# First cross attention: values projected in their own batch, keys a batch ahead, first context and weights split beside the query projection

## The reference

```python
def _L0_xattn_ref(Q, K, V, mask, Wq, bq, Wk, bk, Wv, bv, Wo, bo):
    q = _split_heads(Q @ Wq + bq)          # 16 heads of 32
    k = _split_heads(K @ Wk + bk)
    v = _split_heads(V @ Wv + bv)
    logits = jnp.einsum('bhqd,bhkd->bhqk', q, k) / jnp.sqrt(jnp.float32(DEPTH))
    logits = logits + mask * -1000000000.0
    attn = jax.nn.softmax(logits, axis=-1)
    ctx = jnp.einsum('bhqk,bhkd->bhqd', attn, v)
    ctx = ctx.transpose(0, 2, 1, 3).reshape(Q.shape[0], Q.shape[1], DIM)
    return ctx @ Wo + bo
x = x + _L0_xattn_ref(_layernorm(x, axis=-1), ctx_1024, ctx_1024, mask, ...)
```

## Time and profile before

| | |
|---|---|
| median of three runs | 1742.85 us |
| the profiled execution | 1742.32 us |
| its span | 1740.5 us |
| busy: TensorE / VectorE / ScalarE / GpSimd | 1498.8 (86%) / 1121.7 (64%) / 594.0 (34%) / 295.8 (17%) us |
| first cross attention with query projection | 19.7 to 664 us of the span |
| mean granted clock of TensorE | 0.939 of 2.4 GHz |

### The profile page before, as it was taken

How to read it: one execution, slowest core, us unless ns; L and a number is a source line. 1 busy time by engine, 2 the same in 40 slices (tenths; PEclk the granted TensorE clock), 3 DMA queues, 4 the chain that set the end, 5 groups by cost and what they waited for, 6 DMA issues and landing times. The chain is left out here.

```text
span 1740.5 us, 34070 instructions
## 1 busy us (share of the span) xinstructions
PE 1498.8 (86%) x14116; PEld 989.4 (57%) x14130; DVE 1121.7 (64%) x2155; ACT 594.0 (34%) x1221; POOL 295.8 (17%) x185
## 2 busy tenths in 40 slices
PE   6789999999999975997675999998799995885786
PEld 3567777777777753344644444444466663675343
DVE  3366777667777666614876677574588883665575
ACT  1244444444444431231033111101466661044332
POOL 0400000000000000400010000000599982160000
PEclk9889999999999987899788999998899997898899
DMA  6113123231331214000005000000454521004001
GB/s 233 62 39 133 64 90 94 71 125 64 98 97 60 77 39 138 0 0 2 4 1 200 0 0 0 0 0 0 188 206 168 199 70 35 1 3 146 0 0 48
DMA packets 47910, 120.05 MB, mean 69 GB/s; under 512 B 10606, under 2 KB 15470, under 8 KB 43675
## 3 DMA queue, kind: packets, MB, share of 16 engines
q1 hardware_dynamic: 47770, 118.04, 19.9%
HBM read 100.95 MB, written 17.07 MB: 68 GB/s over the span
## 5 line engine op out<-in xcount | busy, mean ns | idle before, releaser
L1134 POOL TENSOR_TENSOR tm_mixed<-tm_mixed,XNT 128x512 f32<-128x512 f32 x16 | 21.8, 1383 | 648.6 <-DVE tm_mixed L1157 648.6
L478 PE MATMUL bank<-l0x_ctxT,l0x_upper_k 128*128 128x512 f32 x256 | 107.7, 421 | 5.1 <-ACT l0x_upper_k L627 5.1
L697 DVE TENSOR_SCALAR l0x_upper<-bank 128x512 int32<-128x512 int32 x64 | 44.0, 688 | 97.9 <-PE bank L460 92.4
L617 ACT ACTIVATE l0x_ctxT<-l0x_upper 128x512 fp32r<-128x512 f32 x64 | 40.4, 631 | 193.4 <-DVE l0x_ctxT_lower L700 193.4
L478 PE MATMUL bank<-l0x_upper_v,l0x_ctxT 128*128 128x512 f32 x256 | 105.6, 412 | 0.0
L478 PE MATMUL bank<-l0x_ctxT,l0x_lower_k 128*128 128x512 f32 x256 | 101.8, 398 | 0.0
L478 PE MATMUL bank<-l0x_ctxT_lower,l0x_upper_k 128*128 128x512 f32 x256 | 101.6, 397 | 0.0
L478 PE MATMUL bank<-l0x_upper_v,l0x_ctxT_lower 128*128 128x512 f32 x256 | 100.8, 394 | 0.0
L478 PE MATMUL bank<-l0x_lower_v,l0x_ctxT 128*128 128x512 f32 x256 | 100.4, 392 | 0.0
L634 ACT ACTIVATE l0x_prob<-l0x_prob,l0x_negmax 128x512 f32<-128x512 f32 x128 | 91.8, 717 | 17.6 <-DVE l0x_negmax L712 17.6
L1047 DVE TENSOR_REDUCE l1x_negmax<-bank 128x1 f32<-128x512 f32 x128 | 82.3, 685 | 21.3 <-PE bank L936 20.8
(11 more groups left out here) (264 smaller groups left out, 3363.4 us busy)
## 6 DMA issues: line engine op xcount, KB each, us to landing
l0x_ctx<-in_ctx SPq DMA_DIRECT2D x16, 1024.0 KB, 4.9
l1x_ctx<-in_ctx SPq DMA_DIRECT2D x16, 1024.0 KB, 5.8
fp_weight<-l0x_weight_piece SPq DMA_DIRECT2D x24, 352.0 KB, 2.5
f_raw<-fp_weight SPq DMA_DIRECT2D x3, 2816.0 KB, 17.4
ternary_weight<-l1x_piece_out SPq DMA_DIRECT2D x24, 256.0 KB, 6.1
f_raw<-ternary_weight SPq DMA_DIRECT2D x3, 2048.0 KB, 13.9
l0x_abs_piece<-in_L_ffn_w_gate SPq DMA_DIRECT2D x8, 512.0 KB, 5.7
l0x_mask<-mask_scratch SPq DMA_DIRECT2D x16, 256.0 KB, 3.8
```

The source lines that it names most:

```text
L478: last = nc.tensor.matmul(work[bank][:, :], stationary, moving, start=kc == 0 and i == 0, stop=kc == CH - 1 and i == 2)
L697: nc.vector.tensor_scalar(upper.bitcast(I32), work[bank][:, :].bitcast(I32), UPPER_BITS, None, ALU.bitwise_and).then_inc(ctx_upper, 1)
```

## The change

1. In `query_projection` TensorE also turns the four chunks of context 0, one after each of the query chunks 2 to 5, in two PSUM banks that the queries give up (they use six banks, and the last two chunks wait for the first two to be copied). VectorE splits Wk and Wv after the first two query chunks and context 0 after the next four; GpSimd's subtractions, ScalarE's rounding of Wk and of context 0 lie there too. The rounding of Wv is ScalarE's first step in the attention. The splits use the buffers of V, Wo takes the place of Wq.
2. Ahead of the loop stand only the four keys of batch 0 and two turns of context 1. Batch b now computes its own four values in its first half and the four keys of batch b + 1 in its second half. The four context turns are spread: two of context b + 1 in the first half, two of context b + 2 in the second.
3. The scores come half a batch at a time at the start of each half, and the four masked scores and four exponentials of a half stand together in their engines' queues; before they came two and two between other steps. The value product of the second half and the sums' turn come after the first value chunk of the next batch.
4. VectorE's quantising and magnitudes keep their amounts per step, at new places. All order is unrolled over b; SyncE's loop too.

The core of the diff (the waits and addresses that only follow the new counts are left out):

```diff
 def query_projection(nc, g, w):
...
+            for i, (weight, lower) in enumerate(((w.Wk, w.lower_k), (w.Wv, w.lower_v))):
+                pool.wait_ge(w.upper_done, i + 1)
+                nc.gpsimd.tensor_tensor(lower[:, :, :], weight[:, :, :], w.raw_upper[i], ALU.subtract).then_inc(w.lower_done, 1)
...
             for j in range(8):
...
+                if j >= 6:
+                    pe.wait_ge(done, j - 5)
...
+                if TURNS_AFTER <= j < TURNS_AFTER + CH:
+                    turn(j - TURNS_AFTER)
...
+            act.wait_ge(w.lower_done, 1)
+            nc.scalar.activation(w.upper_k[:, :, :], w.raw_upper[0], ACT.Copy).then_inc(w.weights_ready, 1)
+            for c in range(CH):
+                act.wait_ge(w.ctx_lower, c + 1)
+                nc.scalar.activation(w.ctxT[0][:, c, :], w.upper[:, :], ACT.Copy).then_inc(w.ctxt_ready, 1)
...
+                if j < 2:
+                    weight_upper(j, (w.Wk, w.Wv)[j])
+                elif TURNS_AFTER <= j < TURNS_AFTER + CH:
+                    context_parts(j - TURNS_AFTER)
...
+def work_order():
+
+    order = [("key", 0, p) for p in range(CH)] + [("turn", 1, 0), ("turn", 1, 1)]
+    for b in range(B):
+        order += [("value", b, 0), ("value", b, 1), ("turn", b + 1, 2), ("value", b, 2), ("turn", b + 1, 3), ("value", b, 3)]
+        order += [("key", b + 1, 0), ("key", b + 1, 1), ("turn", b + 2, 0), ("key", b + 1, 2)]
+        order += [("out", b // 2 - 1, 0)] if b % 2 == 0 and b > 0 else []
+        order += [("turn", b + 2, 1), ("key", b + 1, 3)]
+        order += [("out", b // 2 - 1, 1)] if b % 2 == 0 and b > 0 else []
+    order += [("out", TILES - 1, 0), ("out", TILES - 1, 1)]
+    return [use for use in order if use[0] == "out" or use[1] < B]
...
         @block.sync
...
+            for b in range(B):
+                it = b // 2
+                if b % 2 == 1:
+                    piece(it, 1)
+                if b + 3 < B:
+                    context_load(b + 3)
+                if b + 2 < B:
+                    mask_load(b + 2)
+                if b % 2 == 0:
+                    piece(it, 0)
+                else:
+                    abs_load(3 * it + 1)
+                    abs_load(3 * it + 2)
+                    piece(it, 2)
...
         @block.tensor
...
+            for b in range(B):
+                scores(b, 0)
+                value(b, 0)
+                if b > 0:
+                    half_product(b - 1, 1)
+                    turn_sums(b - 1)
+                turn_probabilities(b, 0, 0)
+                value(b, 1)
+                turn_probabilities(b, 0, 1)
+                turn(b + 1, 2)
+                value(b, 2)
+                turn_probabilities(b, 0, 2)
+                turn(b + 1, 3)
+                if b < LAST:
+                    value(b, 3)
+                    turn_probabilities(b, 0, 3)
+                    scores(b, 1)
...
+                key(b + 1, 0)
+                half_product(b, 0)
+                turn_probabilities(b, 1, 0)
+                key(b + 1, 1)
+                turn_probabilities(b, 1, 1)
+                turn(b + 2, 0)
+                key(b + 1, 2)
+                turn_probabilities(b, 1, 2)
+                if b % 2 == 0 and b > 0:
+                    out(b // 2 - 1, 0)
+                turn(b + 2, 1)
+                key(b + 1, 3)
+                turn_probabilities(b, 1, 3)
+                if b % 2 == 0 and b > 0:
+                    out(b // 2 - 1, 1)
...
         @block.scalar
...
+                exponentials(b, 0)
+                if b > 0:
+                    sums_copy(b - 1)
+                turned_copy(b, 0, 0)
+                turned_copy(b, 0, 1)
+                context_upper(b + 1, 2)
+                turned_copy(b, 0, 2)
+                context_upper(b + 1, 3)
+                turned_copy(b, 0, 3)
+                exponentials(b, 1)
+                key_copy(b + 1, 0)
+                turned_copy(b, 1, 0)
+                key_copy(b + 1, 1)
+                turned_copy(b, 1, 1)
+                context_upper(b + 2, 0)
+                key_copy(b + 1, 2)
+                turned_copy(b, 1, 2)
+                context_upper(b + 2, 1)
+                key_copy(b + 1, 3)
+                turned_copy(b, 1, 3)
...
         @block.vector
...
+                it, k0 = b // 2, (b % 2 * 4 + s - FIRST_SLOT) * STEPS_A_SLOT
...
+                i = b % 2 * 4 + s - (2 * DOUBLES - 3)
...
+                masked_scores(b, 0)
+                value_copy(b, 0)
+                if b > 0:
+                    finish_heads(b - 1)
+                quantising(b, 0)
+                value_copy(b, 1)
+                context_parts(b + 1, 2)
+                value_copy(b, 2)
+                context_parts(b + 1, 3)
+                if b < LAST:
+                    value_copy(b, 3)
+                    quantising(b, 1)
+                    magnitudes(b, 1)
+                    masked_scores(b, 1)
...
+                spread_sums(b)
+                quantising(b, 2)
+                magnitudes(b, 2)
+                context_parts(b + 2, 0)
+                if b % 2 == 0 and b > 0:
+                    add_out(b // 2 - 1, 0)
+                context_parts(b + 2, 1)
+                quantising(b, 3)
+                magnitudes(b, 3)
+                if b % 2 == 0 and b > 0:
+                    add_out(b // 2 - 1, 1)
```

More of the change, by code:

```diff
@@ L344, in projected_attention, with filled, emptied @@
     ctx_dram = context(d)
[L345 to L370, removed]
+    order = work_order()
+    place = {use: n for n, use in enumerate(order)}
+    LAST = B - 1
+    def filled(what, b, i):
+        n = place[what, b, i]
+        return work[n % 2], work_full[n % 2], n // 2 + 1
+    def emptied(what, b, i):
+        if what == "out":
+            return x_done, 2 * b + i + 1
+        return {"turn": ctxt_ready, "key": key_ready, "value": value_ready}[what], CH * b + i + 1
     with nc.Block() as block:
@@ new lines, in value @@
+            def value(b, p):
+                if p == 0:
+                    pe.wait_ge(weights_ready, 2)
+                bank, full = bank_for("value", b, p)
+                cols = slice(p * P, (p + 1) * P)
+                for kc in range(CH):
+                    c, c_lower = w.ctxT[b % 2][:, kc, cols], w.ctxT_lower[b % 2][:, kc, cols]
+                    nc.tensor.matmul(bank[:, :], c, w.upper_v[:, kc, :], start=kc == 0, stop=False)
+                    nc.tensor.matmul(bank[:, :], c, w.lower_v[:, kc, :], start=False, stop=False)
+                    last = nc.tensor.matmul(bank[:, :], c_lower, w.upper_v[:, kc, :], start=False, stop=kc == CH - 1)
+                last.then_inc(full, 1)
@@ L609, in _, with out @@
-            for it in range(BODIES):
-                body(it, it == 0, it == BODIES - 1)
+            def out(t, j):
+                if j == 0:
+                    pe.wait_ge(w.weight_loaded[2], 16)
+                    pe.wait_ge(heads_done, 2 * t + 2)
+                bank, full = bank_for("out", t, j)
+                for c in range(CH):
+                    last = nc.tensor.matmul(bank[:, 0:256], w.headsT[:, c, :], w.Wo[:, c, j * 256:(j + 1) * 256],
+                                            start=c == 0, stop=c == CH - 1)
+                last.then_inc(full, 1)
@@ new lines, in _ @@
+            for p in range(CH):
+                key(0, p)
+            turn(1, 0)
+            turn(1, 1)
+            for b in range(B):
[15 more added lines that the diff above has]
+                    scores(b, 1)
+                else:
+                    turn_probabilities(b, 0, 3)
+                    scores(b, 1)
+                    value(b, 3)
+                key(b + 1, 0)
[13 more added lines that the diff above has]
+                    out(b // 2 - 1, 1)
@@ L612, in _ @@
+            half_product(LAST, 1)
+            turn_sums(LAST)
+            out(TILES - 1, 0)
+            out(TILES - 1, 1)
         @block.scalar
         def _(act):
[L614 to L622 removed]
@@ L680, in _ @@
-            for it in range(BODIES):
-                body(it, it == 0, it == BODIES - 1)
+                key_copy(0, p)
+            context_upper(1, 0)
+            context_upper(1, 1)
+            for b in range(B):
+                exponentials(b, 0)
[18 more added lines that the diff above has]
+                turned_copy(b, 1, 3)
```

509 lines of the change are left out of this document (192 added, 317 removed).

## The result

The kernel after takes 1747.29 us in the median of 12 runs (1745.62 to 1749.48), the kernel before 1742.68 in 12 runs. The ratio is 1.0027, its 95% interval 1.0019 to 1.0036: slower by 0.27%, where the forecast was 0.13% faster. The profiled execution took 1746.88 us, 4.6 more than that of before.

The account below looks back on a forecast made before the run. TensorE was taken to set the pace, its waits lost time. A start 26.7 us earlier, less 10.9 of moved value projections and 3.1 a pair, with end and restarts, gave - 2.2 us: 1740.5 us, range 1727 to 1752.

Parts of the forecast that it names:

- The start: Query projection to first scores: first key projection at 50.6 instead of 60.20, first scores at 63.0, 26.7 us earlier.
- The cover under the query projection: Weight splitting and context parts lie under the query matmuls, 15 us to spare; up to 4.5 if lost.
- rival D: Split under the query projection does not finish or the first batch starves, 5 to 8 us lost: 1747; chance 0.11.
- The waits: TensorE waits on VectorE's in-order queue in the steady batches: 5.3 us in an odd batch, 0.8 in an even one.
- Rival B: Steady batches cost no more than before, VectorE's order read too pessimistically: 1717, half of it 1729; chance 0.20 for 1717 to 1735.
- The work of a pair: TensorE's work in two steady batches with their output, from step prices: 68.8 us.
- the restart: TensorE resuming after a wait costs about 0.06 more than priced; three more waits, + 0.2 a pair.
- the price of 2.72 for a projection: TensorE's key and value projections: 3.24 with four transposes ahead, less 0.52 for those, leaves 2.72 us.
- The clock: TensorE in the steady batches: full clock expected, half clock after waits left to a rival.
- Rival C: Odd batch's 2.3 us wait drops TensorE's clock, about 1.7 each, + 12 in all seven: 1752; chance 0.17.
- The end: Last batches: batch 14 takes 35.8, batch 15 to the next stage 40.4, with a magnitudes load of 3.7.
- The sum: Next stage at 660.6 against 664.06, - 3.5; restarts + 1.3; in all - 2.2, so 1740.5 us.

Follow-up runs that it names:

- Run 6: Kernel before with only the start changed (first context and weights split beside the query projection), old batch order: 1730.99 us, ratio 0.9937.
- Run 4: Kernel after with the five quantising steps that head an odd batch moved to the end of the even one: 1742.79 us, ratio 0.9993.
- run 5: Kernel after without the sums of magnitudes of batches 1 to 14 and their loads: 1726.26 us, ratio 0.9900.
- Run 1: Kernel after with eight unused matmuls filling TensorE's wait before the second context turn in odd batches: 1746.38 us, ratio 1.0010; second execution 1747.71 us.
- runs 3, 5 and 7: Kernel after with: context parts first and odd batches' last key copy ahead (1734.42 us); magnitudes of batches 1 to 14 omitted (1726.26); VectorE's whole queue rearranged (1713.14).

## Why the prediction was wrong, by its own steps

**The start: right.** First projection 50.6 forecast, 50.17 measured; first scores 63.0 and 62.77; first turned probabilities 68.5 and 68.51; batch 1's scores 97.2 and 97.32. The cover under the query projection held, and rival D is out. Run 6 prices the part alone.

**The waits: right in kind and cause, too long in sum.** In the odd batch I gave 1.2 to the value copy, 1.1 to the exponential, 2.3 to the context turn, 0.47 to the scores; idle times are 1.23, 0.78, 2.13 and 0.34. In the even batch I gave 0.8 and it waits 0.25. Together that is 6.1 forecast and 4.68 measured. Run 4 takes the first away by moving the quantising steps, run 5 the next two by leaving the magnitudes out, work that the forecast named. Rival B, that the order on VectorE is less strict than I read it, is out: 75.5, not 72.

**The work of a pair: a failed step, half hidden by luck.** I had 75.1 a pair with the restart, undisturbed pairs take 75.55, only 0.45 more. But two errors offset each other in it. I took the work as 68.8 in either order, and it measures 69.05 before and 70.88 after: 2.1 too low. The waits and restarts, 6.1 + 0.2, were 1.6 too high. What was mis-sized is the price of 2.72 for a projection wherever it stands. That was 3.24 less a full 0.52 for the transposes ahead; from start to start these take 0.36 and the projection 2.88. In the new order two projections a batch stand straight behind scores, at 2.98, which gives 4 x 0.26 = 1.0 a pair, and eight have a context turn ahead as well, most at 3.84 for both turns and the projection (298.00 to 301.84) instead of 3.76, which gives some 0.6. Where the last 0.5 lies is not traced. Net, over batch 0 and six pairs, it is 0.35 + 6 x 0.45 = 3.1 us by batch 14.

**The clock: the other failed step, put at nothing in the sum.** Rival C had the right place (the wait of 2.3 in the odd batch) and nearly the right price (1.7 each, measured 77.10 - 75.55 = 1.55). But I let it count only if more than half of the odd batches drop, and left it out of the sum. Three of seven dropped: 3 x 1.55 = 4.6 us, the largest single miss. Run 1 shows it from the other side: with the gap filled, batch 14 starts 4.2 and 3.6 us earlier than at 593.24. It should have stood in the sum as a part of the drops, since the earlier trace rows had one long wait with a drop and one without. The Trainium skill ("TensorE: Matmul & The Clock Gate", Part 1, The HAM clock gate) has the clock follow how busy the engine has lately been; that filling the gap with work that computes nothing brings back 1.00 agrees with it, in both executions of run 1's kernel.

**The end: one load under-priced.** Batch 14 took 35.6 (35.8 forecast). The magnitudes' load that is issued behind the last but one sum landed 4.6 us later, where I took 3.7, and its start was 0.2 later; from the last batch's scores (628.80) to the next stage it was 41.6 against 40.4. Together + 1.0.

**The sum.** Forecast for the next stage's first instruction 661.9; - 0.2 (start) + 3.1 (work and waits) + 4.6 (drops) + 1.0 (end) = 670.4, measured 670.44. That is 6.4 behind before. The later stages took 1.8 less in this execution; the two executions of run 1's kernel differ by 6.6 there, so it lies within scatter, but its cause is not shown. 1742.32 + 6.4 - 1.8 = 1746.9, the profiled time. The forecast was 26.7 gained less 24.5 lost, a small difference of large terms, so its sign hung on terms of 3 to 5 us, and the chance of slower, 0.25, was too small for that. Neither failed step is alone to blame: the drops carry 1740.1 to 1744.7, the other terms (- 0.2 + 3.1 + 1.0) carry it to 1744.0, and each is past the 1742.32 of before. Run 1's kernel bears this out: without a drop its next stage still starts 2.4 and 3.4 us behind the earlier trace rows. How many drops the other eleven runs of the kernel after had is not known.

Slips that change little: the largest wait before is the 1.07 at 309.28 and not the 0.95, and the pair waits 2.7, not 3.0; 7 x 0.2 is 1.4, not 1.3; the query matmuls take the 27.7 of the earlier trace rows, not 27.4.

## What to carry to other kernels

When a tuned engine is handed work in a new order, rearrange the queues of the engines that serve it too: side work that nobody waits for goes behind each result that somebody does, and the queue of the engine in between has to let the urgent copy pass (here a pair fell from 75.5 to 70.6 us with not one instruction removed). Price a step by what stands ahead of it, and check waits and work each against the trace: here a sum that was 0.45 off hid 2.1 and 1.6. The waits of 2 us on TensorE cost their own length and, some of the time, 1.5 us more of slow clock, so such a wait is to be priced with a share and not as all or nothing. Where a change gains in one place and loses in another, try the gain alone: the splits beside the query projection were worth 0.6% without the rest.

## What the runs showed of the hardware

The same wait of 2.1 us, with the same instructions around it, dropped TensorE's clock in three of seven batches in two executions and in one of seven in a third that had started 2.4 us later; the wait of 2.1 to 2.2 in run 4 dropped it in five of seven. After a drop the 128x512 matmuls start 0.43 us apart instead of 0.23 for some eight of them. Eight matmuls that compute nothing, 2.1 us in all, were enough to keep the clock at 1.00 in both executions of run 1's kernel. From start to start a projection of twelve took 2.77 behind another, 2.88 behind four transposes and 2.98 behind scores, and the transposes between two projections 0.36. And a query projection with a granted clock of 0.86 from 19 to 31 us started the whole layer 2.4 us late in one of three executions of the kernel after (first scores 65.20 against 62.77); the profiled executions of runs 3, 5 and 7 have the same 0.86 there, and first scores at 64.93 to 65.60.
